# Edge MLP loop: the order of VectorE's queue, edge one-hots moved behind the row addition and the collection

## The reference, cut to what matters

```python
row, col = edge_index                      # source and target of each edge
msg_in = concatenate([x[row], x[col], edge_features], axis=1)   # 128 + 128 + 64
h = relu(msg_in @ W1.T + b1)
messages = h @ W2.T + b2
agg = segment_sum(messages, col, num_segments=3125)
```

## Time and profile before

| | |
|---|---|
| median of 3 runs | 3163.74 us (3162.93 to 3164.66) |
| the profiled execution, its own time | 3167.22 us |
| span of its trace | 3165.5 us |
| the edge loop in it, first to last row addition | 812.6 to 1556.7 us |

### The profile page before, as it was taken

One profiled execution on the slowest core, in us unless ns is written; L12 is line 12 of the kernel. 1 busy time (PEld: TensorE's weight loads), 2 busy tenths in 40 slices (PEclk: granted clock), 3 DMA queues, 4 the chain that ended last, 5 costly groups with the idle time before them and its releaser, 6 DMA issues. The chain is left out here.

```text
span 3165.5 us, 49218 instructions
## 1 busy us (share of the span) xinstructions
PE 2539.5 (80%) x9732; PEld 1562.5 (49%) x9733; DVE 1709.8 (54%) x5128; ACT 866.2 (27%) x2011; POOL 1351.8 (43%) x1326
## 2 busy tenths in 40 slices
PE   3577588987667777677779988996998599999997
PEld 1233344554566666666445444543544455555555
DVE  7999622223544544454342573366257466666665
ACT  1233232222111111111111112113111266666663
POOL 2100000000455555555327735771775177666661
PEclk9999877776555555555579998998999755555556
DMA  0000000002333333322201101110111322222220
GB/s 8 3 0 0 22 0 0 0 0 46 96 83 81 83 83 83 81 83 82 73 26 17 18 9 12 17 16 5 17 18 13 112 64 61 57 58 58 57 58 31
DMA packets 198946, 129.02 MB, mean 41 GB/s; under 512 B 137259, under 2 KB 182107, under 8 KB 197746
## 3 DMA queue, kind: packets, MB, share of 16 engines
q0 software_dynamic: 40224, 60.17, 8.4%
q1 hardware_dynamic: 152745, 59.97, 7.7%
q10 hardware_dynamic: 5803, 7.08, 0.8%
HBM read 107.59 MB, written 13.34 MB: 38 GB/s over the span
## 5 line engine op out<-in xcount | busy, mean ns | idle before, releaser
L1526 PE MATMUL ps<-adj,small 125*128 (+1 forms) x3150 | 631.5, 357 | 0.0
L1251 POOL DMA_INDIRECT edge_rows<-pay,small x425 | 513.6, 1208 | 129.2 <-issue 127.1
L924 POOL DMA_INDIRECT work<-p_rows,small x416 | 394.0, 947 | 355.5 <-DVE work L999 263.1
L1700 POOL DMA_INDIRECT adj<-h_rows,adj x416 | 396.1, 952 | 186.7 <-issue 100.6
L1086 PE MATMUL ps<-small,work 128*128 128x64 f32 x1024 | 277.9, 427 | 221.1 <-issue 217.4
L1526 PEld LDWEIGHTS ps<-adj,small 125*128 125x128 bf16 x3150 | 311.0, 99 | 275.3 <-issue 12.6
L1086 PEld LDWEIGHTS ps<-small,work 128*128 128x128 f32 x1024 | 237.2, 322 | 288.9 <-DVE small L988 176.8
L988 DVE TENSOR_SCALAR small<-work 128x64 f32<-128x64 f32 x512 | 147.1, 328 | 343.9 <-PE ps L1086 343.2
L1075 PE MATMUL ps<-work 128*128 x1024 | 300.4, 449 | 13.7 <-DVE work L983 13.7
L1871 PEld LDWEIGHTS ps<-adj 128*128 128x128 f32 x928 | 214.8, 322 | 154.1 <-issue 98.1
L1033 ACT ACTIVATE work<-work 128x256 f32<-128x256 f32 x256 | 106.7, 417 | 664.4 <-DVE work L999 664.4
(11 more groups left out here) (309 smaller groups left out, 3261.5 us busy)
## 6 DMA issues: line engine op xcount, KB each, us to landing
work<-dst_all SPq DMA_DIRECT2D x256, 64.0 KB
work<-edge_attr SPq DMA_DIRECT2D x256, 64.0 KB
edge_rows<-pay,small POOLq DMA_INDIRECT x425, 2.7
work<-p_rows,small POOLq DMA_INDIRECT x416
adj<-h_rows,adj POOLq DMA_INDIRECT x416
adj<-adj SPq DMA_DIRECT2D x232, 24.0 KB
pay<-edge_pay SPq DMA_DIRECT2D x106, 46.9 KB
work<-x_kept SPq DMA_DIRECT2D x2, 1562.5 KB, 6.5
```

Of the source, the lines that this page charges most:

```text
L924: eng.indirect_dma_start(gathered[:, at:at + D], None, p_rows[:, :], bass.IndirectOffsetOnAxis(ap=src_i[:, c:c + 1], axis=0)).then_inc(s_g ...
L1251: eng.indirect_dma_start(edge_rows[:, :], bass.IndirectOffsetOnAxis(ap=place[:, k:k + 1], axis=0), pay[:, k * ROW:(k + 1) * ROW], None).th ...
L1526: ins = eng.matmul(ps[:, j, 0:cw], parts[k][:, i * D:(i + 1) * D], cols, start=first and i == 0, stop=last and i == 2, skip_group_check=True)
L1700: eng.indirect_dma_start(gathered[:, at:at + D], None, h_rows[:, :], bass.IndirectOffsetOnAxis(ap=row3_i[:, c, DST_C:DST_C + 1], axis=0)). ...
```

## The change

The function `hots` is cut in two. `by_node(v)` waits for the edge data and makes the node one-hots; `by_edge(v, word)` waits for the totals of visit v - 2 and makes the edge one-hots. In turn v of the loop VectorE's queue is then `by_node(v + 1)`, `add(v)`, `collect(v - 1)`, `by_edge(v + 1)`. The instructions, their waits and their buffers stay as they are, and so do the queues of the other engines.

```diff
-            def hots(v, word):
-                b, c = v % KB, column_of(word)
+            def by_node(v):
+                b = v % KB
                 eng.wait_ge(s_km[b], 32 * (v // KB + 1))
                 eng.tensor_scalar(kmat[b][0:MW, :], kmat[b][0:MW, :].bitcast(I32), node[:, 0:1], tile_v[0:MW, v:v + 1],
                                   ALU.subtract, ALU.is_equal).then_inc(s_ht, 1)
+
+            def by_edge(v, word):
+                c = column_of(word)
                 if v >= 2:
                     eng.wait_ge(s_tot, v - 1)
                 for k in range(PAIR):
...
             words = visits_of(eng, 0, 8)
-            hots(0, words[0])
+            by_node(0)
+            by_edge(0, words[0])
             for v in range(VISITS):
...
                 if v + 1 < VISITS:
-                    hots(v + 1, words[v + 1])
+                    by_node(v + 1)
                 add(v, words[v])
                 if v:
                     collect(v - 1, words[v - 1])
+                if v + 1 < VISITS:
+                    by_edge(v + 1, words[v + 1])
             collect(VISITS - 1, words[VISITS - 1])
```

## The result

The changed kernel takes 2942.7 us (median of 4 runs, 2940.8 to 2947.3), the kernel before 3164.2 us beside it. The ratio is 0.9299, 95% interval 0.9283 to 0.9316: 221.5 us less, against 222 forecast (2942, with a range of 2932 to 3003). The profiled execution took 2940.8 us with a span of 2939.1 us.

What follows compares the result with a forecast made beforehand. GpSimd's gathers were to bound the edge loop: 520 us against TensorE's 493 and VectorE's 462. The last gather moves from 1546.8 to 1324.8, so 3163.7 - 222 = 2941.7, said as 2942 us, range 2932 to 3003.

Steps and rivals of the forecast that it cites:

- The old circle: Edge loop before the change: edge one-hots wait for the previous totals, ahead of the addition; 2.90 us a visit.
- step 1: VectorE's queue in the changed loop: circle through the addition now spans two visits, 3.46 us, 1.73 each.
- step 2: TensorE's own queue in the edge loop: 1.85 us a visit plus 32 register loads, 493 us.
- step 3: Node one-hots to products in the edge loop: ready at 2.68 us against 2.73, cover 0.05, no loss.
- step 4: Three edge-data buffers: landing at most 3.00 us, 1.67 a visit; rival that this ring binds, 3098 us, chance 0.10.
- step 5: GpSimd's gathers in the edge loop: 416 steps of 1.25 us, 520 us, becoming the bound.
- Two-visit pairs absorbed: Four gather slots carry the 48 two-visit pairs without loss; rival, not absorbed, 3000 us, partly or wholly 0.22.
- late landing: Gathered rows landing at worst 6.27 us after their start, costing the edge loop at most 26 us; none taken.
- The sum: Whole kernel: last gather at 1324.8 instead of 1546.8, gain 222 us, median 2942; tail left as it was.
- One-hots and gathers exclude each other: Rival in the edge loop: VectorE's one-hots delay GpSimd's gathers, 3.72 us a pair, total 3194; chance of slower 0.04.
- The prediction's sign of being wrong: In the edge loop: the whole forecast is wrong if a gather lasts well over 0.94 us under one-hots.
- Clock: TensorE's granted clock stays at 0.50 in the edge loop; if it rose, GpSimd's 520 us would still decide.

Runs made afterwards that it cites:

- four kernels of the study: Kernel before with three edge one-hot buffers; changed kernel with two-pair gather ring, extra GpSimd memset, or three edge one-hot instructions; on slower chip 3510, 3534, 3528, 3531 us.

## Why the prediction was right, point by point

- *The old circle, 2.90 a visit through the buffer of the edge one-hots.* Right, and shown twice: with half the gathers it doesn't move, and with a third buffer it is gone without the new order.
- *VectorE's circle, 1.73 a visit (step 1).* Not the bound: more one-hot instructions cost nothing. With half the gathers two additions are 1.73 apart in the median, so the size seems right.
- *TensorE's queue, 493 us (step 2).* Too long. A visit's eight matmuls take 1.70 back to back, not 1.85, and the whole loop, register loads and remaining waits included, takes 466.3 once the gathers are halved. It didn't matter to the sum, since GpSimd's term is larger; it did to the margin, which is at least 52 us and not 27.
- *The node path, cover 0.05 (step 3).* No loss in its place: products wait 21.3 us for the node one-hots, 13.6 of them once ahead of the loop. That products can be held by it is shown by moving the node one-hots last, 216 us, and with half the gathers where the clock was 1.00.
- *The ring of edge data, landing at most 3.00 (step 4).* The bound was too low. It came from one transfer in a quiet stretch. Node one-hots now do wait for that transfer, 10.3 us in 22 times. In the changed kernel the targets of visit 5 are issued at 811.44, and the one-hot of that buffer, which waited for the edge features sent behind them, starts at 815.51:

```profile
811.44 0.47 SPq L893 DMA_DIRECT2D work<-dst_all  x1
...
815.51 0.40 DVE L983 TENSOR_SCALAR work<-work 64x256 f32<-64x256 int32 x1 [0.60 <-DMA work<-edge_attr]
```

  That is 4.07. If all took so long, this circle would be (1.40 + 4.07 + 0.62) / 3 = 2.03 a visit, just the pace of the loop. They don't: the 22 that were waited for took 2.83 to 4.75, and with the same ring and half the gathers the loop runs at 1.83. But this ring has less room than I wrote, and no run changes its size.
- *GpSimd's gathers, 520 us (step 5).* Right: 521.5 for 415 steps. Shown from both sides, by fewer gathers and by a longer queue.
- *Two-visit pairs absorbed.* Right: with four pairs no gap ahead of a gather that is put down to an addition is longer than 0.3, and all steps together exceed 1.249 each by 3 us. The 26 us kept in the range for a late landing weren't needed, since the landing is 2.4 to 4.0 where it is told, and not 6.27.
- *The sum.* 222 us against 221.5. The tail after the last gather shrank from 9.9 to 3.8 us (1322.8 to 1326.6), which I had left out of the sum, and the gathers took 521.5 and not 519.1 (1.257 a step, not 1.25), which took 2.4 of the 6.1 back. So the trace shows 225.6 for the loop; that the medians differ by 221.5 lies within the spread of the runs.
- *One-hots and gathers exclude each other.* That this costs next to nothing was right; the reading behind it was partly luck. The one-hots of the steady turn didn't lie inside the gather: the first began 0.14 us before it (1450.22 and 1450.36), and both had ended 0.45 us into it.

  It matters where in a gather they start. In the loop before, 5 of 768 one-hot instructions started 0.43 to 0.60 us behind a gather's start; in the changed one 112 did, and nearly all of those are long. The timeline above has one: the node one-hot at 1103.12, 0.51 behind the gather of 1102.61, takes 0.55, while none that began in the first 0.38 us of a gather took over 0.41. Of the 38 node one-hots among the 112, 34 end 1.05 or 1.06 behind the gather's start, wherever they began. So there is a stretch of some 0.2 us in a gather that shuts a one-hot out. An estimate, from 1.05 less the usual 0.40, puts its end at 0.65.

  VectorE pays 6 us in all on the node one-hots (up to 648 ns, mean 422, before 399). Gathers stay at 944 ns in the median, but 11 of them, the first left out, take 1.02 to 1.08 us, where none did before; one runs with a node one-hot that began ahead of that stretch, and its step is 1.37 instead of 1.25:

```profile
806.65 1.07 POOL L924 DMA_INDIRECT work<-p_rows,small  x1 [0.30 <-issue]
806.82 0.40 DVE L983 TENSOR_SCALAR work<-work 64x256 f32<-64x256 int32 x1
808.02 0.94 POOL L924 DMA_INDIRECT work<-p_rows,small  x1 [0.30 <-DMA work<-p_rows,small]
```

  Most of the other long gathers run beside an addition; what lengthens them isn't shown. The Trainium skill, page "SBUF — State Buffer", section "Who interferes with whom", says that whoever issues first gets the shared ports for the whole instruction. The trace agrees that one waits for the other, and not for the whole instruction, as one-hots that start in the first 0.38 us of a gather aren't delayed. The prediction's sign of being wrong, gathers well over 0.94 us under one-hots, came in single ones, too few for the sum.
- *Clock.* I said 0.50 throughout. Nearly: 0.51 over the loop. That it wouldn't matter was right: with the edge one-hots ahead of the collection and with three buffers the granted clock was 0.56 between 815 and 1325 us, and the times are 2943.9 and 2945.9 us.

## What to carry to other kernels

In a hand-written queue, ask of each wait what stands behind it without needing it: here one instruction's place ahead of another was worth 7% of the kernel, and one more buffer would have been worth the same. When such a circle is opened, take the next bound from the queue with the steadiest steps elsewhere in the same trace (GpSimd's 1.25 at the loop's start), and count it by its own unit, pairs and not visits. Where two engines may disturb each other, look at the moments at which they meet: a steady rhythm can keep them apart, and the change moves the rhythm. A landing time that no row shows as awaited is bounded by a row, not known from it; take it from a stretch as busy as the one you predict.

## What the runs showed of the hardware that I had not expected

- TensorE's granted clock rises now and then in a loop that had been at the lower level throughout. In 100 us windows it was 0.50 before; in the changed kernel it was 0.50 and then 0.52, with matmuls covering 90 to 93 us; with half the gathers 0.50, 0.53 and 0.59, with 94 to 97 us. Within these it is at one of two levels: with half the gathers 0.50 from 1006 to 1008 us and 1.00 from 1010 to 1014. In the last stage, where matmuls covered 199.4 of 200 us, it was 0.50. Two windows of the changed kernel:

```profile
900.00:1000.00 100.00, 92.68 (x396) 87.13 (x396) 72.69 (x248) 20.39 (x49) 75.62 (x81) 0.50 0.44 118
1000.00:1100.00 100.00, 91.01 (x395) 85.64 (x395) 72.20 (x246) 20.52 (x50) 75.73 (x80) 0.52 0.45 119
```

- A memset between two indirect DMAs of GpSimd costs 0.08 us of its 0.22, as it fits into their gap.
- An indirect DMA of GpSimd and a one-hot of VectorE meet in one short stretch of the DMA, some 0.43 to 0.65 us behind its start, and not over its 0.94 us.
- One chip ran the kernel before at 3561 us instead of 3165, and four kernels of the study at 3510 to 3534. In the last one's loop there are 42 stretches of over 1 us, 5.7 us at most, in which TensorE, VectorE and ScalarE all stood between 815 and 1320 us; in the changed kernel's own trace there is none. Two of these kernels take 2946 us elsewhere, 220 less than the kernel before; there they were 30 and 50 less.
